# The last sample group of a DLRM tower kernel: third layer and top network in two parts, 96 samples inside tile 15 and 32 after it

## The reference

```python
e = stack([tbl_f[ids[:, f]] for f in range(39)], axis=1)      # 512 x 39 x 16
x0 = xk = e
for W in (f0, f1, f2):                                        # 39*39 x 128, 128*39 x 128, 128*39 x 128
    z = einsum('bfd,bgd->bfgd', x0, xk).reshape(b, f * g, d)
    xk = einsum('bpd,pm->bmd', z, W)
    outs.append(xk)
z = sum(concatenate(outs, axis=1), axis=-1)                   # 512 x 384
h = concatenate([z, dense_ctx], axis=1)                       # 512 x 400
h = maximum(h @ W_top1 + b_top1, 0)                           # 512 x 512
h = maximum(h @ W_top2 + b_top2, 0)                           # 512 x 256
y = h @ W_top3                                                # 512 x 1
```

## Time and profile before

| | |
|---|---|
| median of 3 runs | 817.92 us (817.79 to 822.41) |
| the profiled execution, its own time | 821.62 us |
| its span in the trace | 819.6 us |
| PE busy, DVE busy, POOL busy, ACT busy (share of span) | 90%, 82%, 61%, 35% |
| mean granted TensorE clock | 0.981 of 2.4 GHz |
| last matmul of `layer2` starts | 788.42 us |
| last copy of the result (ACT) | 817.80 to 818.07 us |

### The profile page before, as it was taken

One profiled execution on the slowest core, in us unless ns is written; L12 is line 12 of the kernel. 1 busy time (PEld: TensorE's weight loads), 2 busy tenths in 40 slices (PEclk: granted clock), 3 DMA queues, 4 the chain that ended last, 5 costly groups with the idle time before them and its releaser, 6 DMA issues.

```text
span 819.6 us, 11557 instructions
## 1 busy us (share of the span) xinstructions
PE 738.6 (90%) x3366; PEld 581.9 (71%) x3366; DVE 674.4 (82%) x2209; ACT 285.0 (35%) x786; POOL 500.1 (61%) x515
## 2 busy tenths in 40 slices
PE   0987999989999999989999999988998999999977
PEld 0975777767677877767677876767777876767657
DVE  4853989988997589988997589987998579999960
ACT  2313333334342234433442233433343243334311
POOL 6886888765785467765785467744464345555330
PEclk9997999999999999999999999999999999999989
DMA  9730000000000000000000000000000000000000
GB/s 225 166 119 3 3 4 4 3 3 3 2 4 2 2 2 4 3 1 4 3 2 3 2 4 2 3 1 0 2 1 1 0 1 1 0 2 1 1 1 1
DMA packets 13101, 12.06 MB, mean 15 GB/s; under 512 B 3952, under 2 KB 11856, under 8 KB 12785
## 3 DMA queue, kind: packets, MB, share of 16 engines
q1 hardware_dynamic: 8494, 10.15, 4.6%
q0 software_dynamic: 4544, 1.17, 1.4%
HBM read 11.31 MB, written 0.00 MB: 14 GB/s over the span
## 4 chain that ended last, share of the span: by engine, by line
PE 39%; DVE 34%; POOL 16%; issue 9%; ACT 2%; DMA 0%; POOLq 0%; ACTq 0%; DVEq 0%
DVE acc L568 23%; POOL emb L305 8%; PE y L689 8%; PE y L691 7%; PE y L690 7%; PE side L707 5%; POOL z_parts L315 4%; DVE z L534 4%; PE acc L671 2%; DVE diag L576 2%; POOL sum L330 2%; DVE acc L565 2%; PE side L718 2%; PE rep L659 1%; DVE x_lo L540 1%
## 5 line engine op out<-in xcount | busy, mean ns | idle before, releaser
L568 DVE SCALAR_TENSOR_TENSOR acc<-y,x_rows,acc 128x128 f32<-128x128 f32 x1856 | 503.3, 340 | 75.6 <-PE y L691 74.9
L689 PE MATMUL y<-w_hi,x_hi 128*128 128x512 f32 (+1 forms) x640 | 273.1, 427 | 2.1 <-DVE x_lo L540 1.6
L691 PE MATMUL y<-w_hi,x_lo 128*128 128x512 f32 (+1 forms) x640 | 250.0, 391 | 0.0
L690 PE MATMUL y<-w_lo,x_hi 128*128 128x512 f32 (+1 forms) x640 | 249.5, 390 | 0.0
L416 ACT ACTIVATE scaled<-y,x_rows 128x128 f32<-128x128 f32 x512 | 145.8, 368 | 243.8 <-PE y L691 237.3
L315 POOL TENSOR_TENSOR z_parts<-z,z_parts 128x512 fp32r<-128x512 f32 x112 | 144.1, 1288 | 54.2 <-ACT z_parts L378 53.9
L305 POOL DMA_INDIRECT emb<-in_tbl_dram,ids_sb x142 | 152.1, 1071 | 32.8 <-issue 20.2
L689 PEld LDWEIGHTS y<-w_hi,x_hi 128*128 128x128 f32 x640 | 121.4, 190 | 35.7 <-DVE acc L568 8.1
L321 POOL TENSOR_TENSOR sum<-scaled 128x512 f32<-128x512 f32 x64 | 82.5, 1290 | 92.8 <-ACT scaled L416 90.9
L691 PEld LDWEIGHTS y<-w_hi,x_lo 128*128 128x128 f32 x640 | 121.0, 189 | 25.5
L690 PEld LDWEIGHTS y<-w_lo,x_hi 128*128 128x128 f32 x640 | 121.6, 190 | 24.5
(11 more groups left out here) (68 smaller groups left out, 557.2 us busy)
## 6 DMA issues: line engine op xcount, KB each, us to landing
w_sb<-in_w_dram SPq DMA_DIRECT2D x1, 2496.0 KB, 9.9
emb<-in_tbl_dram,ids_sb POOLq DMA_INDIRECT x142
s_sb<-in_w_dram SPq DMA_DIRECT2D x12, 160.0 KB
w_sb<-in_small_tables_dram SPq DMA_DIRECT2D x1, 980.0 KB
wt_sb<-in_ids_small_dram SPq DMA_DIRECT2D x1, 896.0 KB
wt_sb<-in_W_top_dram SPq DMA_DIRECT2D x1, 768.0 KB
s_sb<-in_w_dram SPq DMA_DIRECT2D x4, 144.0 KB
scaled<-in_selectors_dram SPq DMA_DIRECT2D x1, 532.0 KB
```

Of the source, the lines that this page charges most:

```text
L568: dve.scalar_tensor_tensor(part, term, x0_f, part, ALU.mult, ALU.add).then_inc(terms_in, 1)
L689: pe.matmul(dst, x1_hi[:, t % 2, cols], hi, start=True, stop=False)
L690: pe.matmul(dst, x1_hi[:, t % 2, cols], lo, start=False, stop=False)
L691: pe.matmul(dst, x1_lo[:, t % 2, cols], hi, start=False, stop=True).then_inc(y_ready, 1)
```

## The change

The last group becomes two parts in a table of five, `HEADS`: (group, first sample, end). Part 3 is the last group's samples 0 to 95, part 4 its samples 96 to 127 (the ones that tile 15 itself makes). Part 3 runs inside tile 15, at the slots L3_LATE = 9 and following, H1_LATE = 20, H2_LATE = 27 and Y_LATE = 32. Part 4 runs behind the loop. Both write the PSUM tensors `rep` and `acc0`, which have no other use in tile 15, instead of `side`. The first top layer of part 4 is split: at slot 35 (PRE_LATE) `last_top1(0)` writes zeros (a 512-column matmul of `ident` and `tick`) and adds the first layer's share, `last_top1(3)` the dense share; behind the loop `last_top1(1)` and `last_top1(2)` add the other two. The copy `r2_out` of the last group falls away, since its 40th row is read from `s_sb` directly. The matmuls have 96 or 32 moving columns instead of 128, and the weights are the same.

```diff
+HEADS = ((0, 0, P), (1, 0, P), (2, 0, P), (3, 0, 96), (3, 96, P))
+LAST = len(HEADS) - 1
+L3_LATE = 9
+H1_LATE = 20
+H2_LATE = 27
+Y_LATE = 32
+PRE_LATE = 35
-            sp.wait_ge(o_in, GROUPS)
+            sp.wait_ge(o_in, len(HEADS))
+        def third_bank(p):
+            return side if p < LAST - 1 else rep
+        def top1_bank(p):
+            return side if p < LAST - 1 else acc0
 # ACT, slots of tile 15
+                    if t == TILES - 1:
+                        if s == L3_LATE + L3_SLOTS:
+                            r3_out(LAST - 1)
+                        if s == H1_LATE + 4:
+                            h1_out(LAST - 1)
+                        if s == H2_LATE + 2:
+                            h2_out(LAST - 1)
+                        if s == Y_LATE + 1:
+                            y_out_of(LAST - 1)
 # PE
-            def layer3(g, fields):
+            def layer3(p, fields):
+                g, lo, hi = HEADS[p]
                 if fields[0] == 0:
-                    pe.wait_ge(s_in, (g + 1) * TPG * NBLK)
+                    pe.wait_ge(s_in, g * TPG * NBLK + hi // BLK)
...
                 for f in fields:
-                    mm = pe.matmul(side[:, 0:P], w2_sb[:, f, :], s_sb[:, f, :], start=f == 0, stop=f == F - 1)
+                    mm = pe.matmul(third_bank(p)[:, 0:hi - lo], w2_sb[:, f, :], s_sb[:, f, lo:hi],
+                                   start=f == 0, stop=f == F - 1)
+            def last_top1(i):
+                g, lo, hi = HEADS[LAST]
+                if i == 0:
+                    pe.wait_ge(h1_in, LAST)
+                    pe.wait_ge(nearly, 1)
+                    pe.matmul(acc0[:, :], ident[0:1, :], tick[0:1, 0:1].to_broadcast([1, COLS]), start=True, stop=False)
+                    x = r1_sb[:, g % 2, lo:hi]
+                elif i == 1:
+                    x = s_sb[:, F, lo:hi]
+                elif i == 2:
+                    pe.wait_ge(r3_in, LAST + 1)
+                    x = r3_sb[:, lo:hi]
+                else:
+                    x = dense_sb[:, g * P + lo:g * P + hi]
+                rows = 16 if i == 3 else P
+                for c in range(H1 // P):
+                    mm = pe.matmul(acc0[:, c * P:c * P + hi - lo], wt1_sb[0:rows, i, c * P:(c + 1) * P], x,
+                                   start=False, stop=i == 2 and c == H1 // P - 1)
+                if i == 2:
+                    mm.then_inc(h1_ready, 1)
+                    if t == TILES - 1:
+                        at = s - L3_LATE
+                        if 0 <= at < L3_SLOTS:
+                            layer3(LAST - 1, range(F * at // L3_SLOTS, F * (at + 1) // L3_SLOTS))
+                        if 0 <= s - H1_LATE < 4:
+                            top1(LAST - 1, s - H1_LATE)
+                        if 0 <= s - H2_LATE < 2:
+                            top2(LAST - 1, s - H2_LATE)
+                        if s == Y_LATE:
+                            top3(LAST - 1)
+                        if s == PRE_LATE:
+                            last_top1(0)
+                            last_top1(3)
             for k in range(LAST_BLOCKS, BLOCKS):
                 pe.wait_ge(s_in, k)
                 s_block(k)
-            layer3(g, range(F))
-            for c in range(4):
-                top1(g, c)
+            layer3(LAST, range(F))
+            last_top1(1)
+            last_top1(2)
             for c in range(2):
-                top2(g, c)
-            top3(g)
+                top2(LAST, c)
+            top3(LAST)
```

More of the change, by code:

```diff
@@ L433, in r2_out, with r3_out, h1_out, h2_out @@
                 copy(r2_sb[:, :], s_sb[:, F, :])
[L435 to L440, removed]
+            def r3_out(p):
+                lo, hi = HEADS[p][1:]
+                act.wait_ge(r3_ready, p + 1)
+                copy(r3_sb[:, lo:hi], third_bank(p)[:, 0:hi - lo]).then_inc(r3_in, 1)
+            def h1_out(p):
+                lo, hi = HEADS[p][1:]
+                act.wait_ge(h1_ready, p + 1)
                 for c in range(H1 // P):
-                    done = act.activation(h1_sb[:, c, :], side[:, c * P:(c + 1) * P], ACT.Relu, bias=bt1_sb[:, c:c + 1])
+                    done = act.activation(h1_sb[:, c, lo:hi], top1_bank(p)[:, c * P:c * P + hi - lo], ACT.Relu,
+                                          bias=bt1_sb[:, c:c + 1])
                 done.then_inc(h1_in, 1)
-            def h2_out(g):
-                act.wait_ge(h2_ready, g + 1)
+            def h2_out(p):
+                lo, hi = HEADS[p][1:]
+                act.wait_ge(h2_ready, p + 1)
                 for c in range(H2 // P):
-                    done = act.activation(h2_sb[:, c, :], side[:, c * P:(c + 1) * P], ACT.Relu, bias=bt2_sb[:, c:c + 1])
+                    done = act.activation(h2_sb[:, c, lo:hi], third_bank(p)[:, c * P:c * P + hi - lo], ACT.Relu,
+                                          bias=bt2_sb[:, c:c + 1])
                 done.then_inc(h2_in, 1)
-            def y_out_of(g):
-                act.wait_ge(o_ready, g + 1)
-                copy(y_sb[:, g * P:(g + 1) * P], side[0:1, 0:P]).then_inc(o_in, 1)
+            def y_out_of(p):
+                g, lo, hi = HEADS[p]
+                act.wait_ge(o_ready, p + 1)
+                copy(y_sb[:, g * P + lo:g * P + hi], third_bank(p)[0:1, 0:hi - lo]).then_inc(o_in, 1)
             act.wait_ge(small_in, 32)
@@ L492, in _ @@
                         s_out(k)
-                        if k % (TPG * NBLK) == TPG * NBLK - 1:
+                        if k % (TPG * NBLK) == TPG * NBLK - 1 and k < BLOCKS - 1:
                             r2_out(k // (TPG * NBLK))
@@ L508, in _ @@
                             y_out_of(g - 1)
+                    if t == TILES - 1:
[7 more added lines that the diff above has]
+                            y_out_of(LAST - 1)
             for k in range(LAST_BLOCKS, BLOCKS):
                 s_out(k)
[L511 to L515, removed]
+            r3_out(LAST)
+            h1_out(LAST)
+            h2_out(LAST)
+            y_out_of(LAST)
         @block.vector
@@ L698, in s_block @@
                           start=True, stop=True).then_inc(s_ready, 1)
-            def layer3(g, fields):
+            def layer3(p, fields):
+                g, lo, hi = HEADS[p]
                 if fields[0] == 0:
-                    pe.wait_ge(s_in, (g + 1) * TPG * NBLK)
+                    pe.wait_ge(s_in, g * TPG * NBLK + hi // BLK)
                     pe.wait_ge(w2_in, 16)
-                    if g > 0:
-                        pe.wait_ge(r3_in, g)
+                    if p > 0:
+                        pe.wait_ge(r3_in, p)
+                    if p == LAST:
+                        pe.wait_ge(o_in, p)
@@ L706, in layer3, with top1 @@
                 for f in fields:
-                    mm = pe.matmul(side[:, 0:P], w2_sb[:, f, :], s_sb[:, f, :], start=f == 0, stop=f == F - 1)
+                    mm = pe.matmul(third_bank(p)[:, 0:hi - lo], w2_sb[:, f, :], s_sb[:, f, lo:hi],
+                                   start=f == 0, stop=f == F - 1)
                 if fields[-1] == F - 1:
                     mm.then_inc(r3_ready, 1)
-            def top1(g, c):
+            def top1(p, c):
+                g, lo, hi = HEADS[p]
                 if c == 0:
-                    pe.wait_ge(r3_in, g + 1)
+                    pe.wait_ge(r3_in, p + 1)
@@ L714, in top1 @@
                     pe.wait_ge(r1_in, TPG * (g + 1))
                     pe.wait_ge(top_in, 112)
[L716 to L719, removed]
+                dst, cut = top1_bank(p)[:, c * P:c * P + hi - lo], slice(c * P, (c + 1) * P)
@@ L720, in top1 @@
+                r2 = r2_sb[:, :] if g < GROUPS - 1 else s_sb[:, F, lo:hi]
+                for i, x in enumerate((r1_sb[:, g % 2, lo:hi], r2, r3_sb[:, lo:hi])):
+                    pe.matmul(dst, wt1_sb[:, i, cut], x, start=i == 0, stop=False)
+                mm = pe.matmul(dst, wt1_sb[0:16, 3, cut], dense_sb[:, g * P + lo:g * P + hi], start=False, stop=True)
                 if c == H1 // P - 1:
                     mm.then_inc(h1_ready, 1)
-            def top2(g, c):
+            def last_top1(i):
[18 more added lines that the diff above has]
+                    mm.then_inc(h1_ready, 1)
@@ L724, in top2 @@
+            def top2(p, c):
+                lo, hi = HEADS[p][1:]
                 if c == 0:
-                    pe.wait_ge(h1_in, g + 1)
-                cut = slice(c * P, (c + 1) * P)
+                    pe.wait_ge(h1_in, p + 1)
                 for i in range(H1 // P):
-                    mm = pe.matmul(side[:, cut], wt2_sb[:, i, cut], h1_sb[:, i, :], start=i == 0, stop=i == 3)
+                    mm = pe.matmul(third_bank(p)[:, c * P:c * P + hi - lo], wt2_sb[:, i, c * P:(c + 1) * P],
+                                   h1_sb[:, i, lo:hi], start=i == 0, stop=i == 3)
@@ L729, in top2, with top3 @@
                 if c == H2 // P - 1:
                     mm.then_inc(h2_ready, 1)
-            def top3(g):
-                pe.wait_ge(h2_in, g + 1)
```

(9 more changed lines are left out.)

## The result

| | before | after |
|---|---|---|
| median | 818.08 us (817.79 to 822.41) | 837.92 us (836.98 to 839.68) |
| span of the profiled execution | 819.6 us | 835.8 us |
| slot 9's bank done to last bank done | 25.0 us | 42.9 us |
| last bank done to `s_block` 63 | 4.5 us | 3.4 us |
| `s_block` 63 to the end of the result's copy | 25.0 us | 26.8 us |

The changed kernel is slower: 1.023 of the time before (95% interval 1.020 to 1.026). From slot 9's end to the copy of the result it takes 73.1 us instead of 54.5, which is 18.6 more. The two spans differ by 16.2 only, because in the profiled executions slot 9 of tile 15 ends 2.5 us earlier after (761.12) than before (763.61). No instruction that runs before that differs, and executions of one kernel spread by some us, so I compare from slot 9 on. The medians differ by more, 19.8 us.

The account below looks back on a forecast made before the run. DVE was taken to bound tile 15, with 3.1 us free on PE for 19.7 of moved work. `s_block` 63 at 808.5 plus a 28.0 us tail ends 18.4 us later; added to the median, 836.3 us, range 823 to 841.

Parts of the forecast that it names:

- the likeliest case: Behind the loop, part 4 runs at 1.2 GHz from layer 3 on; 836.3 us in total, chance 0.75.
- its two halves: Tile 15: 19.7 us of moved work against 3.1 free on PE; tail: full weight loads at 1.2 GHz, 28.0 us.
- Which engine bounds tile 15: Tile 15: DVE sets the pace before, PE having 3.1 us free; after the change PE does from slot 9 on.
- The narrow price inside the tile: Tile 15: weight loads pace narrow matmuls, 0.107 us per record for 96 and 32 columns alike; layer 3 adds 8.8 us.
- The length of the tile: Tile 15: 19.7 us added on PE, 3.1 free, so the last bank ends at 805.2 instead of 788.6.
- rival 4: Tile 15: clock falls to 0.50 for the last four banks, adding 3 us: 839; an edge of the 0.75 case.
- The gap: Between last bank and `s_block` 63: 3.3 us, of which DVE ends 1.9 after PE and POOL takes 1.4.
- The tail: From `s_block` 63 to the end of the result's copy: 28.0 us against 25.0 before.
- The clock: Tail: granted clock 0.50 from layer 3 on, 0.213 us per record, so 78 records take 16.6 us.
- The rival by which the clock comes back like before: Tail: layer 3 regains full clock after about 22 records; 827 us; chance 0.17 together with a clock never cold.
- Payment by columns: Tile and tail: matmuls cost by moving columns, 0.027 us for 32; 811 to 815 us; chance 0.06.

Follow-up runs that it names:

- 2-field run: The changed kernel, but part 3's layer 3 makes only the first and last of its 39 fields; 831.09 us.
- 128-column run: The changed kernel, but part 4's layer 3 moves all 128 columns per field instead of 32; 831.56 us, 1.014 of before.
- 32- and 64-column runs: The kernel before, with layer 3 behind the loop moving 32 or 64 columns instead of 128; 829.16 and 830.05 us.
- the run with shares and 5 unread matmuls: The kernel before, last group whole, its first top layer in shares, zeroing matmul, 5 unread matmuls in the gap and 4 before `top2`; 812.44 us, 0.993.

## Why the prediction was right

The forecast was 836.3 us, the measurement is 837.92; the likeliest case occurred, by its own mechanism, and each of its two halves was tested by itself (the tile by moving slot 35's work and by the 2 fields, the tail by 128, 64 and 32 columns). Point by point:

- **Which engine bounds tile 15.** Right. DVE had no idle time before and waits 15.2 us for PE's banks after. The 2-field run shows both limits in one tile.
- **The narrow price inside the tile.** Right: 8 records with 96 columns put the next bank off by 0.81 us, against 0.80 with 128. `top1` costs 780.91 - 779.79 = 1.12 per chunk (forecast 1.17), slot 35 799.28 - 796.11 = 3.2 (forecast 3.4; the 16-row ones cost 1.1 together, not 1.6, the other two parts 1.0 each, not 0.9).
- **The length of the tile.** 42.9 us against 41.6. The difference is rival 4, which the sum left out: in the profiled execution the clock fell behind slot 35. Bank 636, the `s_block` and bank 637 took 802.78 - 799.28 = 3.5 us instead of 1.9, so it cost 1.6 us and not the 3 of the rival.
- **The gap.** 3.4 us against 3.3, and that near a hit is in part luck. The forecast's 1.9 us from PE's end to DVE's doesn't come out of its own terms: 15 terms of 0.259, the last one 0.34 long, are 4.0, less the 2.3 before the end 1.7. DVE did end 1.9 us behind PE (805.92 and 804.00), but because it waited once more, 0.89 us, for bank 637, and took its last 11 terms from 802.98 on.
- **The tail.** 26.8 us against 28.0. Layer 3 16.2 to the next line's start (forecast 16.6; its first records still ran at full clock), the top1 parts 3.6 and `top2` 3.6 as forecast. The narrower ACT copies and `top3` were cheaper by 0.6 in all, `s_block` ran at full clock (1.3 with its copy, forecast 1.6).
- **The clock.** Right, and it decides the tail: where it comes back, with 128 columns, the tail is 7.3 us shorter than with 32. The 86 narrow matmuls at the start were the row that told it. The rival by which the clock comes back like before (the first of the list, though the prediction once calls it the second) was tried by the 128-column run, where it does come back, and by the 32- and 64-column runs, where it doesn't. The Trainium skill (TensorE: Matmul & The Clock Gate, Part 1) says that sustained matmul activity releases the throttle; here 16.9 us of unbroken 64-column matmuls did not, so an unbroken run of matmuls is not by itself enough.
- **Payment by columns.** Refuted in both directions, 96 columns at the price of 128 inside the tile, and 128 at less than the price of 32 behind it. (The tail terms of this rival add up to 7.75 us where it has 7.4, which moves its result by 0.4 us.)

The tile took 1.3 us more than its term and the tail 1.2 less. They cancel by luck, so the total is nearer than its parts: the sum gave 18.4 us, the traces from slot 9 on 18.6. Against the 19.8 between the medians it is 1.4 short.

## What to carry to other kernels

A matmul with few moving columns costs its weight load (here 0.81 us for eight records with 96 columns and 0.80 with 128), so splitting a batch repeats every weight load and saves little on the smaller part. Before work is moved under another engine's time, count from starts in the timeline how much time the receiving engine has free there (here 3.1 us for 19.7). Look at the granted clock of a serial tail too: in the kernel before some 10 of the tail's 25 us ran at 1.2 GHz. Give the wait behind the last bank to independent shares of the next layer and to wide matmuls that nobody reads, which here brought 6.9 us together.

## What the runs showed of the hardware that was not expected

- The clock can stay at 1.2 GHz with 128 moving columns too: `top1`, with its 16-row matmuls among the others, ran 9.3 us at 0.50 behind a narrow layer 3, where a 128-column layer 3 came back after 4.3 and 4.5 us. Whether the 16-row matmuls are the reason was not tried.
- It can fall while PE is busy without a pause: behind slot 35 (799.2 to 802.4 at 0.50) and in the gap of the run with shares and 5 unread matmuls. The traces of the two other runs that keep slot 35's work in the tile show the same fall (0.50 from 800.9 to 804.0 with 128 columns, from 793.0 to 796.0 with 2 fields), and the two that move it out have 1.00 in the last 4 us of the tile. Before each fall stands a matmul whose weights have one row, and then narrow or 16-row matmuls. Which of them is the cause stays open.
- The clock column can't be trusted at the start of a trace. It reads 1.00 from 18.5 to 43.8 us in the trace of the kernel before, and the narrow matmuls there stand 0.213 us apart, which goes with 0.50 in every other stretch of these runs.
